# Splitting the second group's x earlier, and the logits' weight sums at the network's first product

## What is computed

```python
h = gelu(cond @ W0 + b0); h = gelu(h @ W1 + b1)
att = softmax(h @ W2 + b2)                       # (64, 8)
agg_w = einsum('bk,koi->boi', att, weight)       # a 32x32 mixer per sample
agg_b = att @ bias_k
m = einsum('boi,bih->boh', agg_w, x) + agg_b[:, :, None]
logits = m @ gate_w.T                            # 8 experts, the best 2 kept, softmax
f = m @ base_w.T + base_b + 2 * sum_e w_e * (m @ A_e.T @ B_e)
```

## Time and profile before

| what | value |
|---|---|
| median of 3 runs | 175.69 us (175.65 to 175.91) |
| the profiled execution, its own time | 175.38 us |
| its span | 173.6 us |
| TensorE busy | 167.0 us, 96% of the span |
| VectorE busy | 124.9 us, 72% |
| GpSimd busy | 94.2 us, 54% |
| ScalarE busy | 86.3 us, 50% |

### The profile page before, as it was taken

The page is one execution under the profiler, slowest core; times in us unless marked ns, Lnnn a source line. Parts: engine busy times, 40 slices in busy tenths (PEclk is TensorE's granted clock), DMA queues, the critical chain, the costliest instruction groups (busy, mean ns, idle before and its releaser), DMA issues.

```text
span 173.6 us, 3104 instructions
## 1 busy us (share of the span) xinstructions
PE 167.0 (96%) x1097; PEld 155.7 (90%) x1097; DVE 124.9 (72%) x259; ACT 86.3 (50%) x204; POOL 94.2 (54%) x98
## 2 busy tenths in 40 slices
PE   7999998999999999999999999999999999999990
PEld 7796787889899999998898999999899999999980
DVE  2546999799955559989995346998997953367661
ACT  5475865985544667533260467322415463236141
POOL 8402409998299999928028299630007696056000
PEclk9999999999999999999999999999999999999999
DMA  5999000544004400000041000000041000000336
GB/s 181 357 398 397 22 0 0 190 135 121 0 0 111 136 0 0 4 0 0 0 180 67 0 0 0 4 0 0 25 161 60 0 0 4 2 0 0 122 123 242
DMA packets 7215, 13.21 MB, mean 76 GB/s; under 512 B 800, under 2 KB 1696, under 8 KB 7200
## 3 DMA queue, kind: packets, MB, share of 16 engines
q1 hardware_dynamic: 6912, 12.75, 21.2%
q10 hardware_dynamic: 288, 0.26, 0.5%
HBM read 8.82 MB, written 4.19 MB: 75 GB/s over the span
## 4 chain that ended last, share of the span: by engine, by line
PE 79%; DVE 11%; ACT 2%; POOL 2%; issue 2%; DMA 1%; DVEq 0%
PE ps L1108 19%; PE ps L1110 18%; PE ps L1109 18%; PE ps L1200 8%; PE ps L1121 2%; POOL xTl L379 2%; PE ps L1138 2%; PE ps L1297 2%; PE ps L1298 2%; DMA xT_s<-in_xT_dram 1%; DVE xsl L797 1%; DVE eq L778 1%; PE ps L1309 1%; DVE xs L929 1%; PE ps L1212 1%
## 5 line engine op out<-in xcount | busy, mean ns | idle before, releaser
L1108 PE MATMUL ps<-xw_h,xTh 128*128 128x264 f32 (+1 forms) x96 | 30.8, 321 | 0.8 <-POOL xTl L379 0.8
L1109 PE MATMUL ps<-xw_l,xTh 128*128 128x264 f32 (+1 forms) x96 | 29.9, 311 | 0.0
L1110 PE MATMUL ps<-xw_h,xTl 128*128 128x264 f32 (+1 forms) x96 | 29.8, 310 | 0.0
L379 POOL TENSOR_TENSOR xTl<-xT_s,xTh 128x512 fp32r<-128x512 f32 x12 | 15.8, 1340 | 15.9 <-ACT xTh L520 7.6
L384 POOL TENSOR_TENSOR zl<-outb,zh 128x340 fp32r<-128x340 f32 x15 | 15.1, 1009 | 14.2 <-ACT zh L555 7.2
L1108 PEld LDWEIGHTS ps<-xw_h,xTh 128*128 128x128 f32 x96 | 18.0, 188 | 1.9 <-POOL xTl L379 1.3
L877 DVE TENSOR_TENSOR outb<-ps,s_sb 128x340 f32<-128x340 f32 x16 | 8.2, 510 | 14.5 <-PE ps L1110 10.8
L1109 PEld LDWEIGHTS ps<-xw_l,xTh 128*128 128x128 f32 x96 | 18.1, 188 | 0.1
L1110 PEld LDWEIGHTS ps<-xw_h,xTl 128*128 128x128 f32 x96 | 18.1, 188 | 0.0
L1200 PEld LDWEIGHTS ps<-mixT,xp 128*128 128x128 f32 x128 | 16.7, 191 | 1.4 <-DVE x1T L864 0.2
L395 POOL TENSOR_TENSOR x1Tl<-x1T,x1Th 128x512 fp32r<-128x512 f32 x12 | 16.6, 1389 | 2.3 <-DVE late L901 2.3
(11 more groups left out here) (232 smaller groups left out, 512.8 us busy)
## 6 DMA issues: line engine op xcount, KB each, us to landing
xT_s<-in_xT_dram SPq DMA_DIRECT2D x16, 256.0 KB, 3.1
out_dram<-outb SPq DMA_DIRECT2D x12, 256.0 KB, 2.2
x1T<-in_wT_dram SPq DMA_DIRECT2D x4, 256.0 KB, 4.7
outb<-in_wrow_dram SPq DMA_DIRECT2D x4, 256.0 KB, 6.6
x1T<-in_az_dram SPq DMA_DIRECT2D x1, 680.0 KB, 8.0
outb<-in_tapw_dram SPq DMA_DIRECT2D x1, 576.0 KB, 3.7
out_dram<-x1T SPq DMA_DIRECT2D x2, 256.0 KB, 2.2
lgw_s<-in_lgw_dram SPq DMA_DIRECT2D x1, 272.0 KB, 4.2
```

Of the source, the lines that this page charges most:

```text
L379: nc.gpsimd.tensor_tensor(lo[:, c, :], xT_s[:, g % 2, c, :], hi[:, c, :].bitcast(F32), ALU.subtract).then_inc(x_lo, 1)
L1108: nc.tensor.matmul(dst, sh, mh, start=start and c == 0, stop=False)
L1109: nc.tensor.matmul(dst, sh, ml, start=False, stop=False)
L1110: last = nc.tensor.matmul(dst, sl, mh, start=False, stop=stop and c == n - 1)
```

## The change

TensorE makes the sum of the logits' weights (old line 1371) right behind the network's first product, ahead of the first logits, and waits for ScalarE's copy of it before the attention's bias product. The base product's chunk 1 runs for two tiles, not one, before the attention's transpose, and for the other two behind the spreading.

ScalarE copies that sum between the network's two gelus. It makes the high parts of group 1's x in chunks 0 and 1 before it copies the attention, chunk 2 before it places the mixer, and chunk 3 after that.

GpSimd makes the low parts of chunks 0 and 1 before its first bias rows, chunk 2 right after them, and chunk 3 once the base weights' low parts are complete. Its wait for `lb_lo` is gone. The semaphores `x_hi` and `x_lo` are split by the parity of the group.

```diff
-        x_hi, x_lo, xl_mm, ... = (...)
+        x_hi, x_lo = [sem(f"x_hi{a}") for a in range(2)], [sem(f"x_lo{a}") for a in range(2)]
...
             def x_low(g, c):
-                pool.wait_ge(x_hi, DC * g + c + 1)
+                pool.wait_ge(x_hi[g % 2], DC * (g // 2) + c + 1)
...
             nc.gpsimd.tensor_tensor(lgw_t[:, 2, :], lgw_t[:, 0, :], lgw_t[:, 1, :], ALU.add).then_inc(lgt_ok, 1)
+            x_low(1, 0)
+            x_low(1, 1)
             pool.wait_ge(in_mixw, 16)
             pool.wait_ge(attT_ok, 1)
             bias_rows(0)
+            x_low(1, 2)
+
             pool.wait_ge(base_lo, DC)
-            x_low(1, 0)
-            x_low(1, 1)
-            pool.wait_ge(lb_lo, 1)
-            x_low(1, 2)
             x_low(1, 3)
             bias_rows(1)
...
             nc.scalar.activation(h1T[:, :], ps[:, HID, 0:NB], ACT.Gelu, ...).then_inc(h1_ok, 1)
+            act.wait_ge(lgsum_mm, 1)
+            nc.scalar.activation(lg_sum[:, :], lgs_b, ACT.Copy).then_inc(lgsum_ok, 1)
             act.wait_ge(h2_mm, 1)
...
             x_high(0, 2)
             base_high(2)
+            x_high(1, 0)
+            x_high(1, 1)
             act.wait_ge(attT_mm, 1)
             nc.scalar.activation(attT[:, :], attT_b, ACT.Copy).then_inc(attT_ok, 1)
             xl_out(0)
-            act.wait_ge(lgsum_mm, 1)
-            nc.scalar.activation(lg_sum[:, :], lgs_b, ACT.Copy).then_inc(lgsum_ok, 1)
             xl_out(1)
             x_high(0, 3)
             base_high(3)
+            x_high(1, 2)
             act.wait_ge(zero_ok, 1)
             mix_place(0)
-            x_high(1, 0)
-            x_high(1, 1)
+            x_high(1, 3)
             act.wait_ge(zero_ok, 2)
             bias_high(0)
-            x_high(1, 2)
-            x_high(1, 3)
             gate_exp(0, gate0, dif0_ok, ex0_ok)
...
+            pe.wait_ge(consts, 3)
             pe.wait_ge(in_early, 16)
             nc.tensor.matmul(ps[:, HID, 0:NB], ...).then_inc(h1_mm, 1)
+            pe.wait_ge(lgt_ok, 1)
+            nc.tensor.matmul(lgs_b, ones[:, :], lgw_t[:, 2, :], start=True, stop=True).then_inc(lgsum_mm, 1)
             x_logits(0)
...
             x_logits(1)
-            pe.wait_ge(consts, 3)
+            pe.wait_ge(lgsum_ok, 1)
...
             x_base(0, 0, (1,))
+            x_base(0, 1, (1,))
             pe.wait_ge(att_ok, 1)
             nc.tensor.transpose(attT_b, att_n[:, :], ident[0:NB, 0:NB]).then_inc(attT_mm, 1)
             pe.wait_ge(place_ok, 1)
             pe.wait_ge(att_ok, 2)
             nc.tensor.matmul(attb_b, ...).then_inc(attb_mm, 1)
-            x_base(0, 1, (1,))
+            x_base(0, 2, (1,))
+            x_base(0, 3, (1,))
             pe.wait_ge(attT_ok, 1)
-            pe.wait_ge(lgt_ok, 1)
-            nc.tensor.matmul(lgs_b, ones[:, :], lgw_t[:, 2, :], start=True, stop=True).then_inc(lgsum_mm, 1)
-            x_base(0, 2, (1,))
-            pe.wait_ge(lgsum_ok, 1)
             pe.wait_ge(in_mixw, 16)
             nc.tensor.matmul(mixb_b, ...).then_inc(mixb_mm, 1)
-            x_base(0, 3, (1,))
             x_base(0, 0, (2,))
```

More of the change, by code:

```diff
@@ L240, in two_layer_mixer @@
                              "pjsum_mm", "pjsum_ok", "pj_ctx_ok"))
-        x_hi, x_lo, xl_mm, xl_ok, xa_mm, xa_ok, p0_mm, p0_ok, lg_mm, lg_ok, lgw_hi, lgw_lo = (
-            sem(n) for n in ("x_hi", "x_lo", "xl_mm", "xl_ok", "xa_mm", "xa_ok", "p0_mm", "p0_ok", "lg_mm", "lg_ok",
+        xl_mm, xl_ok, xa_mm, xa_ok, p0_mm, p0_ok, lg_mm, lg_ok, lgw_hi, lgw_lo = (
+            sem(n) for n in ("xl_mm", "xl_ok", "xa_mm", "xa_ok", "p0_mm", "p0_ok", "lg_mm", "lg_ok",
                              "lgw_hi", "lgw_lo"))
@@ L376, in x_low @@
             def x_low(g, c):
-                pool.wait_ge(x_hi, DC * g + c + 1)
+                pool.wait_ge(x_hi[g % 2], DC * (g // 2) + c + 1)
                 hi, lo = x_parts(g)
                 nc.gpsimd.tensor_tensor(lo[:, c, :], xT_s[:, g % 2, c, :], hi[:, c, :].bitcast(F32),
-                                        ALU.subtract).then_inc(x_lo, 1)
+                                        ALU.subtract).then_inc(x_lo[g % 2], 1)
             def z_low(p, t):
@@ L519, in x_high @@
                     act.wait_ge(p0_mm, TG * g)
-                nc.scalar.activation(x_parts(g)[0][:, c, :], xT_s[:, g % 2, c, :], ACT.Copy).then_inc(x_hi, 1)
+                nc.scalar.activation(x_parts(g)[0][:, c, :], xT_s[:, g % 2, c, :], ACT.Copy).then_inc(x_hi[g % 2], 1)
             def xl_out(half):
@@ L853, in bias_x @@
                 dve.wait_ge(xT_in[i % 2][c], 16 * (i // 2 + 1))
-                dve.wait_ge(x_lo, DC * i + c + 1)
+                dve.wait_ge(x_lo[i % 2], DC * (i // 2) + c + 1)
                 if i == 0:
@@ L936, in x_low @@
             def x_low(c):
-                dve.wait_ge(x_hi, c + 1)
+                dve.wait_ge(x_hi[0], c + 1)
                 hi, lo = x_parts(0)
-                minus(lo[:, c, :], xT_s[:, 0, c, :], hi[:, c, :]).then_inc(x_lo, 1)
+                minus(lo[:, c, :], xT_s[:, 0, c, :], hi[:, c, :]).then_inc(x_lo[0], 1)
             def base_low(c):
@@ L1156, in x_first @@
                 for c in chunks:
-                    pe.wait_ge(x_lo, DC * g + c + 1)
+                    pe.wait_ge(x_lo[g % 2], DC * (g // 2) + c + 1)
                     last = hi_lo(ps[:, P0[t], 0:HX], [(hi[:, c, cols(t)], lo[:, c, cols(t)])],
@@ L1168, in x_base @@
                     if g == 0:
-                        pe.wait_ge(x_lo, c + 1)
+                        pe.wait_ge(x_lo[0], c + 1)
                         pe.wait_ge(base_lo, c + 1)
```

## The result

| | executions | median | from, to |
|---|---|---|---|
| before | 13 | 175.69 us | 175.47 to 176.32 |
| changed | 13 | 177.65 us | 175.75 to 178.22 |

The ratio is 1.0079, 95% interval 1.0054 to 1.0104: slower, clear of noise, and the median lies beyond the stated range (175.0 to 176.5). The median hides the form of it. The thirteen executions of the changed kernel lie in two clusters with nothing between: four from 175.75 to 175.86 us, with a mean granted clock of 0.995 to 1.00, and nine from 177.43 to 178.22 us, with 0.985 to 0.99.

The account below looks back on a forecast made before the run. The prediction took TensorE, busy 160.45 of 162.00 us at full clock, as the bound. A 1.80 us loss less a 1.50 us gain gave +0.30 us on 175.69, so 176.0 us; range 175.0 to 176.5, clock left out.

Parts of the forecast that it names:

- (a): Sum's matmul at the network's first product: attention path 0.245 us later, regained at its old place; net nothing.
- (b): Two chunk 1 tiles ahead of the attention's transpose: transpose and spreading 0.935 us late, including the sum's 0.245.
- (c): ScalarE's early high parts and GpSimd's two low parts before the transpose: fit in idle time, cost nothing.
- (d): At chunk 2, GpSimd's low part blocks VectorE's base subtraction: 1.80 us later, 0.87 from ports; TensorE gap some 2.0 us.
- (e): GpSimd's fourth low part moves to the logits; comparison wins back 1.11 us, gates 0.69 us later but covered: worth nothing.
- (f): Second group's first products no longer wait for low parts: TensorE wins 1.50 us, 1.39 from transposes to mixer.
- (g): After 32 us, gates' transpose 1.69 us later, covered by 1.8 us of ScalarE slack: nothing, else 0 to 0.2 us.
- the likeliest case: Whole kernel: port collision loss and TensorE gain as summed, +0.30 us, spanning 175.8 to 176.2 us; chance 0.50.
- rival 4: Clock falls in TensorE's 2.0 us gap ahead of chunk 2: at most 6.7 us more, 182.7 us; chance 0.03.

Follow-up runs that it names:

- both edits: Changed kernel with GpSimd's chunk 2 low part behind the base low parts' wait and only one chunk 1 tile ahead of the attention's transpose: 174.98 us.
- x early: Kernel before plus only the early split of group 1's x, GpSimd's chunks 2 and 3 after the base weights' low parts: 174.66 us.
- one-tile kernel: Changed kernel with one tile of chunk 1, not two, ahead of the attention's transpose and three behind it: 177.34 us.
- filled kernel: Changed kernel with eight dummy 512-column matmuls in TensorE's gap ahead of chunk 2's first product: 175.93 us.
- chunk 2 late: Changed kernel with GpSimd's low part of chunk 2 moved behind the wait for the base weights' low parts: 175.74 us.
- place first: x early with ScalarE placing the mixer before, not after, converting group 1's chunk 2: 174.73 us.
- turn first: x early with the attention's transpose and spreading ahead of all of chunk 1's products: 175.04 us.
- turn first, free: turn first with the mixer placed first on ScalarE and only one early low part on GpSimd: 175.22 us.
- order alone: Kernel before plus only TensorE's new order and ScalarE's copy of the sum, x split as before: 176.68 us.
- two dummies: Changed kernel with two dummy matmuls in TensorE's gap ahead of chunk 2's first product: 176.11 us.
- gap in x early: x early with two extra VectorE reductions (1.8 us) ahead of chunk 2's base subtraction: 177.88 us.
- gap in the kernel before: Kernel before with two extra VectorE reductions (1.8 us) ahead of chunk 2's base subtraction: 177.66 us.

## Why the prediction was wrong

**(a), (b): right.** The order costs 0.93 us at chunk 2, alone and unhidden; worked out: 0.935. The sum's place costs 0.25 us of it: chunk 2 starts 9.61 us after the network's first product with it (both edits) and 18.42 - 9.06 = 9.36 without (x early); worked out: 0.245.

**(c), (d): right.** GpSimd takes the ports 0.27 us before VectorE comes (17.97 and 18.24), worked out 0.30. Chunk 2's first product starts 11.08 us after the network's, before 9.30: 1.78 us later; worked out: 1.80. The gap is 2.16 us; worked out: some 2.0. The rule of the ports, whoever starts first holds them to the end, fits the durations in all the rows shown here. It does not say who comes next when GpSimd has a second instruction queued: in the one-tile kernel that one went first, in the last kernel VectorE did. What I had not thought of, that the small bias rows hold them too, did not touch the forecast but spoiled two experiments.

**(e): right.** Comparison at 0.41 us, gates covered: in the filled kernel their result comes 0.72 us later than before, worked out 0.69.

**(f): right, a little under.** From chunk 2 to the mixer the undisturbed stretch takes 12.86 us (gap filled) against 32.09 - 17.58 = 14.51: 1.65 us, worked out 1.50. The part from the gates' transposes to the mixer went from 4.76 to 32.59 - 29.20 = 3.39 us: 1.37 of 1.39. Most of the rest is a shorter stretch at the mixed logits. Not all of (f) is there for every kernel: with chunk 2 late, with both edits and with the placing first, where TensorE comes to these products earlier, the stretch takes 13.13 us, and the gain is 1.38.

**(g): right.** The filled kernel keeps its 0.16 us: 161.57 from the network's first product to the end, against 161.41.

So where the clock stays up, the change does nearly what the sum said: +0.16 us in the filled kernel's trace, forecast +0.30; four executions at 175.75 to 175.86, at the lower edge of the likeliest case (175.8 to 176.2).

**The step that failed is rival 4 and its chance.** Step (d) priced the gap of 2.0 us by its length alone, and the sum and the range put the clock at nothing. I forecast the gap that lowers the clock, cited the Trainium skill, which warns of it, and gave it 0.03, because no row showed a fall. That absence was no evidence: the longest wait in the earlier trace rows is 0.6 us (the 0.8 that the prediction names is the sum of two), so the trace had never asked the question. It happened in 9 of 13 executions. The bound that I put on its price, 6.7 us, was as poor: the clock stood low from about 19.8 to 23.2 us, and cost 14.41 - 12.86 = 1.55 us. The gap itself, by contrast, was right. The sum's 176.0 with that cost added is 177.5; the measured median is 177.65, though the close match is in part luck, since the sum is 0.14 us high by the traces and the clusters lie further apart than 1.55. The Trainium skill ("TensorE: Matmul & The Clock Gate", section "HAM oscillation — how this bites in real kernels") warns of idle gaps longer than any in this table. Here the runs decide, and a gap of 1.5 us was enough in a third of the executions. Each gap is that of one profiled execution:

| TensorE's gap ahead of chunk 2 | kernel | clock fell |
|---|---|---|
| none to 0.3 us | x early; place first; turn first; turn first, free | 0 of 6; 0 of 6; 0 of 6; 0 of 8 |
| 0.7 us | both edits | 0 of 12 |
| 1.3 us | chunk 2 late; order alone | 0 of 11; 0 of 7 |
| 1.5 us | two dummies | 4 of 12 |
| 1.9 us | one tile; gap in x early; gap in the kernel before | 8 of 12; 5 of 6; 3 of 5 |
| 2.2 us | the change | 9 of 13 |
| filled | eight dummies | 0 of 11 |

In which executions the clock falls at a given gap stays open; nothing that I varied picks them. Nor is the length shown to be all that counts: the kernels differ in more than it, and the numbers of executions are small.

## What to carry to other kernels

Where TensorE is nearly always busy, price a new gap twice: its length, and the slow stretch that may follow, which here began to appear between 1.3 and 1.5 us of idleness and cost some 1.5 us more. A trace without such a gap says nothing of what the clock would do in one. Before a GpSimd operation is moved earlier, list VectorE's instructions with two SBUF inputs in the window it will land in, and count the small GpSimd operations too. Where the times of one kernel fall in two clusters, read each cluster with its clocks; the median only tells which of them holds more executions.

## What I had not expected of the hardware

A GpSimd operation on 8 partitions holds the ports as one on 128 does: VectorE's 0.68 us subtraction took 1.45 us beside it. And when such an operation ended with another queued directly behind it, the waiting VectorE instruction did not get its turn between them in one kernel: it came at 17.43, the bias rows ended at 17.63, the next subtraction went first, and VectorE's ended at 19.40. In another kernel VectorE's comparison did get in between two GpSimd subtractions; what decides it stays open. Eight matmuls on constants, whose results nobody reads, made the changed kernel's median 1.7 us shorter (177.65 to 175.93).
